# Decoder layer on one core: values ahead of keys in two steps, output projection ahead of half the self scores, second self output a step later

## The reference

```python
x = layernorm(x + self_attn(x))            # 16 heads of 16, rotary, softmax
x = layernorm(x + cross_attn(x, ctx))      # ctx: 375 tokens; 16 heads of 64; own layernorm, gate
x = layernorm(x + moe(x))                  # 8 experts, top 2, and a shared one; swiglu
```

## Time and profile before

| | us |
|---|---|
| median of 3 runs (716.7 to 722.49) | 719.34 |
| the profiled execution | 719.09 |
| its span, first to last instruction | 717.3 |
| the eight passes over b, about | 105 to 530 |
| TensorE busy in the span | 592.4 (83%) |
| VectorE busy | 478.0 (67%) |
| ScalarE busy | 408.7 (57%) |
| mean granted clock of TensorE | 0.925 |

### The profile page before, as it was taken

How to read it: one execution, slowest core, us unless ns; L and a number is a source line. 1 busy time by engine, 2 the same in 40 slices (tenths; PEclk the granted TensorE clock), 3 DMA queues, 4 the chain that set the end, 5 groups by cost and what they waited for, 6 DMA issues and landing times. The chain is left out here.

```text
span 717.3 us, 14307 instructions
## 1 busy us (share of the span) xinstructions
PE 592.4 (83%) x4746; PEld 462.2 (64%) x4746; DVE 478.0 (67%) x903; ACT 408.7 (57%) x995; POOL 268.4 (37%) x296
## 2 busy tenths in 40 slices
PE   4733788999999989989989989999759878899980
PEld 3523566777777777778778777777546564566650
DVE  3895446877877876876876876876747786733332
ACT  2445337567567567567567567565517546644431
POOL 3462023344344344344354354333412741333332
PEclk9965788999999999999999999999966999999995
DMA  8625110210210210210210210310307576333324
GB/s 221 227 101 177 29 49 30 50 51 15 64 49 14 65 51 6 72 43 15 70 41 17 71 40 15 112 59 35 103 30 264 163 246 227 64 59 54 60 30 110
DMA packets 58069, 57.34 MB, mean 80 GB/s; under 512 B 17266, under 2 KB 47218, under 8 KB 58034
## 3 DMA queue, kind: packets, MB, share of 16 engines
q1 hardware_dynamic: 53650, 50.89, 23.1%
q0 software_dynamic: 4384, 5.99, 5.0%
HBM read 46.74 MB, written 10.13 MB: 79 GB/s over the span
## 5 line engine op out<-in xcount | busy, mean ns | idle before, releaser
L652 POOL TENSOR_TENSOR c_rcp<-c_sum,neg_one 112x2 f32<-112x2 f32 x64 | 44.5, 696 | 203.4 <-ACT probs L795 203.4
L656 POOL TENSOR_TENSOR probs<-probs,c_rcp 112x750 f32<-112x750 f32 x64 | 92.0, 1437 | 5.0
L795 ACT ACTIVATE probs<-ps_s,c_neg 112x375 f32<-112x375 f32 x128 | 72.6, 580 | 22.8 <-DVE c_neg L1027 22.3
L687 ACT ACTIVATE kt_hi<-ps_o 128x376 fp32r<-128x376 f32 x64 | 31.8, 497 | 68.3 <-PE ps_o L151 68.3
L1658 POOL DMA_INDIRECT moe_sum<-gsh_hi,xs_in x21 | 34.2, 1628 | 79.4 <-ACT gsh_hi L1709 64.7
L1031 DVE SCALAR_TENSOR_TENSOR cpt_lo<-ps_t,cpt_hi 125x672 f16<-125x672 f32 x64 | 54.4, 850 | 13.0 <-ACT cpt_hi L802 13.0
L1022 DVE SCALAR_TENSOR_TENSOR v_lo<-ps_vx,v_scale,v_hi 125x512 f16<-125x512 f32 x48 | 35.9, 749 | 40.3 <-ACT v_hi L787 39.9
L1347 PE MATMUL ps_t<-ident,probs 112*125 112x112 f32 x384 | 54.4, 280 | 8.8 <-DVE cpt_lo L1031 8.7
L1027 DVE TENSOR_REDUCE c_neg<-ps_s 112x2 f32<-112x750 f32 x64 | 59.4, 929 | 1.1 <-PE ps_s L151 1.1
L1971 PE MATMUL ps_h<-w_ex,xst_hi 128*128 (+1 forms) x168 | 58.0, 387 | 2.5 <-DVE xst_lo L1748 2.4
L1347 PEld LDWEIGHTS ps_t<-ident,probs 112*125 112x125 f32 x384 | 50.4, 195 | 12.6 <-POOL probs L656 7.5
(11 more groups left out here) (312 smaller groups left out, 1796.9 us busy)
## 6 DMA issues: line engine op xcount, KB each, us to landing
chunk<-in_L_ffn_ew_dram SPq DMA_DIRECT2D x24, 512.0 KB, 3.6
spare<-in_L_ffn_ew_dram SPq DMA_DIRECT2D x18, 512.0 KB, 6.1
store<-in_L_ffn_ew_dram SPq DMA_DIRECT2D x6, 512.0 KB, 5.3
ctx_all<-in_ctx_dram SPq DMA_DIRECT2D x2, 1500.0 KB
ctx_raw<-in_ctx_dram SPq DMA_DIRECT2D x8, 375.0 KB
moe_in<-chunk SPq DMA_DIRECT2D x1, 2709.0 KB, 14.1
plain_raw<-in_L_xattn_w_kv_dram SPq DMA_DIRECT2D x2, 1024.0 KB, 15.2
xs_in<-moe_in SPq DMA_DIRECT2D x15, 129.0 KB, 2.1
```

The costliest lines, as they stand in the source:

```text
L652: pool.tensor_tensor(c_rcp[:, s % 2, :], c_sum[:, s % 2, :], neg_one[:, :], ALU.pow).then_inc(sg["c_rcp_ready"], 1)
L656: pool.tensor_tensor(p, p, r, ALU.mult).then_inc(sg["p_normed"], 1)
L795: act.activation(probs[:, s % 2, h, :], ps_s[0:N, h, 0:SK], ACT.Exp, bias=c_neg[:, s % 2, h:h + 1], accum_out=c_sum[:, s % 2, h:h + 1]).th ...
```

## The change

The order of instructions is changed on TensorE, ScalarE and VectorE. No computation is added or taken away, and no buffer changes.

- In steps 3 and 6 (`V_FIRST`) the value projection (V11, and V00 of the next entry) stands ahead of the key projection. ScalarE has there the exps, the value copy, then the key copy; VectorE the value split ahead of the key split.
- In step 2 the output projection stands ahead of the self scores S2 and S3. VectorE takes the maxima of S2 and S3 behind the key split and `x2_moments`.
- O1 moves from the end of step 3 to the place ahead of the key projection in step 4.
- V00 waits for both halves of the next ctx (the key projection ahead of it waited for them before).

```diff
--- before.py
+++ after.py
@@ -87,10 +87,12 @@
 
 FILL_AT = {(0, 2): ["QA"], (0, 3): ["QB"], (0, 4): ["KA"], (1, 0): ["KB"], (1, 3): ["S0", "S1"],
            (2, 1): ["S2", "S3"], (2, 3): ["T0"], (2, 4): ["T1"], (3, 1): ["O0", "T2"],
-           (3, 2): ["T3"], (3, 4): ["O1"], (5, 1): ["OT", "C0"], (5, 3): ["C1", "PJ"],
+           (3, 2): ["T3"], (4, 0): ["O1"], (5, 1): ["OT", "C0"], (5, 3): ["C1", "PJ"],
            (6, 3): ["NT"], (7, 1): ["R0", "R1"], (7, 2): ["Q0", "Q1"]}
 
 V_AT = {0: "V02", 2: "V10", 3: "V11", 4: "V12", 6: "V00", 7: "V01"}
+
+V_FIRST = (3, 6)
 
 
 def v_here(b, s, more):
@@ -864,18 +866,20 @@
 
                     if more and s == 0:
                         stack_hi(b + 1)
-                    if s == 2:
+                    if s == 2 or s in V_FIRST:
                         exps(b, s)
                     place(0)
+                    if s in V_FIRST and v_here(b, s, more):
+                        v_hi_cross(b if s < 6 else b + 1, V_AT[s])
                     if s + 2 < PAIRS:
                         k_hi(b, s + 2)
                     elif more:
                         k_hi(b + 1, s + 2 - PAIRS)
-                    if s in (3, 7):
+                    if s == 7:
 
                         exps(b, s)
                     place(1)
-                    if s not in (2, 3, 7):
+                    if s not in (2, 7) and s not in V_FIRST:
                         exps(b, s)
 
                     if s == 6:
@@ -883,7 +887,7 @@
                         o_hi(b, s - 2)
                         if more:
                             xn_hi(b + 1)
-                    if v_here(b, s, more):
+                    if s not in V_FIRST and v_here(b, s, more):
                         v_hi_cross(b if s < 6 else b + 1, V_AT[s])
                     place(2)
                     if more and s == 0:
@@ -1143,26 +1147,25 @@
                         place(0)
                     if not lo_first and (s >= 2 or later(b)):
                         late_cpt_lo(b, s)
-                    if s == 2:
-                        place(1)
-                    else:
+                    if s != 2:
                         place(0)
+                    if s in V_FIRST and v_here(b, s, more):
+                        v_lo_cross(b if s < 6 else b + 1, V_AT[s])
                     if s + 2 < PAIRS:
                         k_lo(b, s + 2)
                     elif more:
                         k_lo(b + 1, s + 2 - PAIRS)
                     if more and s == 0:
                         stack_lo(b + 1)
-                    if s != 2:
-                        place(1)
                     if s == 2 and later(b):
                         x2_moments(b - 1)
+                    place(1)
                     if more and s == 2:
                         chunk_max(3 * b)
                     if s == 6:
                         o_lo(b, s - 2)
                         place(3)
-                    if v_here(b, s, more):
+                    if s not in V_FIRST and v_here(b, s, more):
                         v_lo_cross(b if s < 6 else b + 1, V_AT[s])
                     place(2)
                     if more and s == 0:
@@ -1314,6 +1317,8 @@
 
             def v_project(b, f):
                 q, t = int(f[1]), int(f[2])
+                if f == "V00":
+                    pe.wait_ge(sg["ctxt_lo"], 2 * b + 2)
                 if f == "V10" and later(b):
 
                     pe.wait_ge(sg["res2"], b)
@@ -1432,14 +1437,16 @@
                     k_done = PAIRS * b + min(s + 3, PAIRS if not more else s + 3)
                     scores(b, s)
                     place(0)
+                    if s in V_FIRST and v_here(b, s, more):
+                        v_project(b if s < 6 else b + 1, V_AT[s])
                     if s + 2 < PAIRS:
                         k_project(b, s + 2)
                     elif more:
                         k_project(b + 1, s + 2 - PAIRS)
-                    place(1)
                     if s == 2 and later(b):
                         cross_out(b - 1)
-                    if s != 2 and v_here(b, s, more):
+                    place(1)
+                    if s != 2 and s not in V_FIRST and v_here(b, s, more):
                         v_project(b if s < 6 else b + 1, V_AT[s])
                     place(2)
                     if s >= 1:
```

## The result

The changed kernel takes 786.11 us (median of 4, 783.25 to 789.37) against 720.91 for the one before (median of 4): the ratio is 1.0908, 95% interval 1.0857 to 1.096. It is slower by 65 us. The forecast was 770 with a range of 742 to 785: the sign was right, the size too small by 16 us, and the time lies just outside the range.

The account below looks back on a forecast made before the run. TensorE, busy 52.08 of 56 us, was taken as the bound. Passes 1 to 6 at 5.6 for waits plus 1.5 for the clock (42.6), pass 0 (7.0) and pass 7 (1.3) gave 50.9 on 719.2: 770 us, range 742 to 785.

Parts of the forecast that it names:

- Bound and direction: Attention loop: TensorE has the most busy time, 52.08 of 56 us; slower by over 1% with chance 0.92.
- Rival (d): Step 6: pv does not wait for VectorE's key split, TensorE's order alone counts, 14 us won, 705; chance 0.04.
- (e): Whole kernel: gains and stalls cancel, 719 us; chance 0.04.
- Step 2, term 0: Output projection's gain is waited for again at T0, term 0; VectorE reaches step 3's maxima 0.60 us late.
- Step 3: T3 waits 2.5 us for O0's sum, behind V11's copy and split; scores of step 4 come 0.97 late.
- Step 6: pv waits 2.3 us for a key split behind V00's copy and split; 1.9 as seen at the query projection.
- Steps 4 and 5: O1 in step 4 makes step 5's scores 1.97 late; OT comes 3.86 late, 1.9 a stall for the transfer.
- All waits together: Passes 1 to 6: the stalls of the steps make each pass end 5.6 us late.
- The clock: Clock falls behind the waits at T3, OT and pv of step 6; only the third is charged, 1.5 us a pass.
- Rival (c): Loop: every low-clock stretch is paid, 10.7 us a pass, 795; chance 0.06.
- Pass 7: Last pass, no next entry: only step 3 counts, pv waits for a key split behind V11's, about 1.3 us.

Follow-up runs that it names:

- s2: Kernel before with only step 2's new order (output projection ahead of S2 and S3, their maxima behind the residual's moments): 725.45 us, ratio 1.0065.
- v6_warm: v6 with 17 extra matmuls, results unused, on TensorE ahead of pv in step 6: 737.54 us, ratio 1.0222.
- o1: Kernel before with only O1 moved to step 4: 733.24 us, ratio 1.0153.
- after_warm: Changed kernel with extra matmuls, results unused: 17 ahead of T3, 10 ahead of OT, 17 ahead of pv in step 6: 765.78 us, ratio 1.0611.
- warm6: Changed kernel with 17 extra matmuls, results unused, ahead of pv in step 6 only: 774.93 us, ratio 1.0743.
- v6: Kernel before with only V00 moved ahead of the key projection in step 6, on all three engines: 747.89 us, ratio 1.0362.
- warm3: Changed kernel with 17 extra matmuls, results unused, ahead of T3 in step 3 only: 777.39 us, ratio 1.079.
- warm5: Changed kernel with 10 extra matmuls, results unused, ahead of OT in step 5 only: 784.88 us, ratio 1.0884.
- v3: Kernel before with only V11 moved ahead of the key projection in step 3, on all three engines: 746.8 us, ratio 1.036.
- pe_only: Whole change on TensorE and O1's move everywhere; ScalarE and VectorE keep the old order of steps 2, 3 and 6: 737.26 us, ratio 1.0243.
- s2_max: s2 with VectorE taking the maxima of S2 and S3 ahead of the residual and its moments again: 724.14 us, ratio 1.0068.

## Why the prediction was right, and where it was wrong

**Bound and direction.** Right. The 2.02 us of waits named for TensorE went, but more came back behind other engines. Rival (d), 14 us won, and (e) are out.

**Step 2, term 0.** Right in kind, and the 0.60 us of lateness on VectorE was 0.47. T0 waits 1.1 us for S2's exps; s2 alone grew the pass by 0.5.

**Step 3.** The wait at T3 was put at 2.5 us (the prediction's own times, 293.39 less 290.70, give 2.69) and is 2.42; its releaser is the one named. T3 comes 2.3 us late, 2.44 was forecast.

**Step 6.** The wait of pv was put at 2.3 and is 2.33, behind a split of kt. Alone, it costs 1.8 us a pass without the clock's part (v6_warm), against 1.9.

**Steps 4 and 5.** The transfer's stall at OT is real: 1.8 us in o1, 1.49 in the pass from 293.97. In the pass from 229.43 and two others it is absent, since step 4 ran at the low clock and TensorE came to OT late itself.

**All waits together** were put at 5.6 us a pass and are 5.3. The chain can be followed in the pass of after_warm from 286.67, which has no fall. Counted from each pass's first scores, the scores of step 4 come 0.83 us later than before (0.97 forecast), those of step 5 1.78 (1.97), OT 3.68 (3.86), pv of step 6 5.91 (6.00), the end of the pass 5.24 (5.6).

**The clock: the step that failed.** The prediction's sentence was that the low clock after the first two gaps "runs into waits on others (the 1.9 at OT covers the first), so I charge them nothing", and that the third costs 1.5. Together the falls cost 4.0 us a pass. The fall at T3 costs 2.2 where 0 was charged (warm6). Two things were wrong: what was to hide it, and its length.

The wait at OT couldn't hide it. OT waits for a transfer that starts when O1 is normalised, and O1 stands behind T3. What the low clock costs up to there delays the transfer as well, and the wait at OT moves along. The store and OT in the pass from 293.97, with a fall of 3.4 us at T3, and in the pass from 483.26, with none:

```profile
329.02 0.33 SPq L581 DMA_DIRECT2D o_shuffle<-o_self  x1
...
333.88 0.41 PE L1263 MATMUL ps_a<-ident,o_rows 112*128 112x112 f32 x2 [1.49 <-DMA o_rows<-o_shuffle]
...
517.16 0.33 SPq L581 DMA_DIRECT2D o_shuffle<-o_self  x1
...
522.02 0.41 PE L1263 MATMUL ps_a<-ident,o_rows 112*128 112x112 f32 x2 [1.72 <-DMA o_rows<-o_shuffle]
```

From the first scores, the store comes at 35.05 us against 33.90 and OT at 39.91 against 38.76. Both are 1.15 later, and nearly the whole wait is still there.

The length was taken from one fall of some 3.4 us. The fall at T3 is 10.2 us in three passes of six, over pv, scores, O1, the key projection and V12. That work took 8.5 us from the scores of step 4 to those of step 5 in the pass from 229.43, against 5.7 in the pass from 293.97. So the wait at OT was used up and TensorE itself came to OT 2.6 us later than in the pass from 483.26. At pv the charge of 1.5 fits a fall of 3.4 us (1.3 to 1.5 in v6), but in the same three passes the fall is 6.8 us, and costs 2.4 to 2.7. What makes one fall three times as long as another no run shows.

With 4.0 instead of 1.5 for the clock and 5.3 for the waits a pass grows by 9.3, the measured 9.2; 7.1 was forecast. Over six passes that is 13 of the 16 us that were missing. Rival (c), every fall paid, with 10.7 a pass and 795 us, was nearer than the forecast.

The Trainium skill, TensorE: Matmul & The Clock Gate (HAM oscillation — how this bites in real kernels), describes a loop whose waits for transfers between bursts of matmuls lower the clock in every turn, so that it is paid in each. The trace agrees, for waits on VectorE of 2.3 and 2.4 us too: 0.87 and 0.92 in two passes that had 1.00 before, and 20 us back when the waits were filled.

**The range.** It ended at 785 because errors of half a microsecond were allowed in each of four terms. A term that was set to zero by an argument (a fall hidden by a wait) deserved its full price at the other end: rival (c) at 795 was to be the upper end.

**Pass 7** was put at 1.3 us and has, with everything behind it, 3.5; what of this is the pass and what is variation behind the loop stays open.

## What to carry to other kernels

When one engine is over 90% busy and two others 68 to 77% (as here in a pass), its small waits are often the distance to the other engines, and an order that removes them on that engine moves them to the next place where it needs a result: look first for instructions that start within 0.1 us of their releaser, since anything put ahead of that releaser is paid almost in full (here 1.8 us of 2.3). On engines that take their list in order, the copy that frees a shared bank goes ahead of long work (here the exps). A wait on TensorE can have a second price, the slower clock behind it. Take that price from the longest fall in the trace, not from the shortest, and don't let a later wait hide it without asking what releases that wait: if its releaser stands behind the slow stretch too, the wait moves along and hides nothing.

## What the runs showed of the hardware

Adding work made a kernel faster: 17 matmuls with unused results in a stall of 2.3 us took v6 from 748 to 738 us, and 44 a pass took the changed kernel from 786 to 766. Falls of the clock were of unequal length at like waits: at T3 (2.4 us) 10.2 us in three passes of the changed kernel, 3.4 in two and none in one.

Shorter waits brought a fall less often. Counted in passes 1 to 6 of the profiled executions are falls that begin between 1.2 us before the wait's end and 1.9 us behind it:

| wait on TensorE | run | passes with a fall there |
|---|---|---|
| pv of step 6, 2.3 us | after, v6, warm3, warm5 | 6 of 6 in each |
| T3, 2.4 us | after | 5 of 6 |
| T3, 2.4 us | warm5, warm6 | 6 of 6 in each |
| T3, 1.9 us | v3 | 6 of 6 |
| OT, 1.6 to 1.8 us | o1 | 5 of 6 |
| OT, 1.7 to 1.8 us | pe_only | 3 of 6 |
| V10, 1.2 us | pe_only | 2 of 6 |
| V10, 1.2 us | s2_max | 1 of 6 |
| T0, 1.1 us | s2 | 0 of 6 |

With the stalls filled, a fall still came in three passes of six, in v6_warm as in after_warm.

Passes without a fall repeat to 0.02 us in after_warm (59.16 to 59.18) and to 0.3 us in the kernel before (53.77 to 54.07).
